# Taking the products that nobody reads out of TensorE's program, in the setup and at the change of layer

## The reference

```
x_n = x_flat / max(norm(x_flat over pixels), 1e-12)
cos = einsum('bcn,bdn->cd', x_n, x_n) / 32
idx = top_k(-abs(cos).T, 2)               # each channel's partner
gs, gsq = sums and square sums of a channel and its partner
x = gamma * (x - mean) * rsqrt(var + eps) + beta
```

```
off1 = make_offset(conv3x3(x, tm1_w, tm1_b), conv3x3(x, tr1_w, tr1_b))
out = relu(batchnorm(deform_conv(x, off1, dcn1_w), bn1_g, bn1_b))
off2 = make_offset(conv3x3(out, tm2_w, tm2_b), conv3x3(out, tr2_w, tr2_b))
out = batchnorm(deform_conv(out, off2, dcn2_w), bn2_g, bn2_b)
return relu(out + x)
```

## Time and profile before

| | before |
|---|---|
| median of 3 runs | 448.58 us (447.6 to 449.65) |
| profiled execution | 447.31 us, of which the span is 445.4 us |
| TensorE busy | 415.5 us, 93% of the span, 7435 records |
| ScalarE, VectorE busy | 318.5 us (72%), 313.4 us (70%) |
| GpSimd busy | 110.6 us (25%) |
| mean granted TensorE clock | 0.990 |

### The profile page before, as it was taken

How to read it: one execution, slowest core, us unless ns; L and a number is a source line. 1 busy time by engine, 2 the same in 40 slices (tenths; PEclk the granted TensorE clock), 3 DMA queues, 4 the chain that set the end, 5 groups by cost and what they waited for, 6 DMA issues and landing times.

```text
span 445.4 us, 18471 instructions
## 1 busy us (share of the span) xinstructions
PE 415.5 (93%) x7435; PEld 308.0 (69%) x7435; DVE 313.4 (70%) x865; ACT 318.5 (72%) x385; POOL 110.6 (25%) x241
## 2 busy tenths in 40 slices
PE   5978999999999999999988999999999999999970
PEld 4755677777777777777865677777777777777860
DVE  4657977777787777776429877877777777777435
ACT  2536787777887777777726788777877778777735
POOL 6203422222222222208002322222222212210000
PEclk9999999999999999999999999999999999999996
DMA  7202332222211122212000242212222222221005
GB/s 224 69 2 45 55 47 44 48 45 45 45 35 30 35 45 45 46 37 39 3 1 6 54 82 37 36 34 44 45 45 45 44 42 41 43 48 37 3 3 189
DMA packets 59385, 20.72 MB, mean 47 GB/s; under 512 B 51680, under 2 KB 59184, under 8 KB 59344
## 3 DMA queue, kind: packets, MB, share of 16 engines
q1 hardware_dynamic: 54464, 17.75, 19.4%
q0 software_dynamic: 4880, 2.37, 2.2%
HBM read 3.24 MB, written 2.10 MB: 12 GB/s over the span
## 4 chain that ended last, share of the span: by engine, by line
PE 88%; ACT 4%; DVE 4%; DMA 1%; issue 1%; SPq 0%; DVEq 0%; ACTq 0%
PE acc_ps L672 57%; PE z_ps L649 13%; PE build_ps L633 10%; PE side_ps L585 3%; PE side_ps L595 2%; ACT S L454 1%; DMA xs<-in_x 1%; PE side_ps L575 1%; ACT raw L507 1%; DVE bstats L764 1%; PE side_ps L615 1%; PE acc_ps L542 1%; PE build_ps L532 1%; ACT conv_sb L431 0%; ACT Z L447 0%
## 5 line engine op out<-in xcount | busy, mean ns | idle before, releaser
L672 PE MATMUL acc_ps<-S,Z 64*64 64x256 f32 x4608 | 286.7, 376 | 1.1 <-ACT S L454 1.0
L454 ACT ACTIVATE S<-build_ps,minus 128x1024 f32<-128x1024 f32 x192 | 203.7, 1111 | 51.6 <-PE build_ps L633 50.7
L672 PEld LDWEIGHTS acc_ps<-S,Z 64*64 64x64 f32 x4608 | 193.7, 132 | 56.4 <-issue 3.8
L649 PE MATMUL z_ps<-wz,xflat 64*64 64x192 f32 x1536 | 109.6, 331 | 0.1
L895 DVE TENSOR_SCALAR S<-build_ps 128x512 f32<-128x512 f32 x96 | 66.1, 689 | 35.2 <-PE build_ps L633 35.1
L447 ACT ACTIVATE Z<-z_ps 128x768 f32<-128x768 f32 x96 | 77.9, 812 | 5.4 <-PE z_ps L649 5.4
L649 PEld LDWEIGHTS z_ps<-wz,xflat 64*64 64x64 f32 x1536 | 71.3, 132 | 12.5 <-issue 0.5
L265 POOL DMA_DIRECT2D moved<-conv_sb x140 | 70.8, 513 | 20.0 <-POOL conv_sb L354 15.8
L633 PE MATMUL build_ps<-feat_rows,cst 64*64 64x512 f16 x576 | 72.1, 381 | 2.9 <-ACT S L454 1.5
L897 DVE TENSOR_SCALAR S<-build_ps 128x512 f32<-128x512 f32 x96 | 65.3, 680 | 0.0
L902 DVE COPY raw<-acc_ps 128x256 f32 (+1 forms) x32 | 13.6, 424 | 67.2 <-PE acc_ps L672 67.2
(11 more groups left out here) (103 smaller groups left out, 260.7 us busy)
## 6 DMA issues: line engine op xcount, KB each, us to landing
xs<-in_x SPq DMA_DIRECT2D x4, 512.0 KB, 6.4
out<-raw SPq DMA_DIRECT2D x7, 256.0 KB, 2.5
moved<-conv_sb POOLq DMA_DIRECT2D x56, 11.2 KB, 1.7
moved<-conv_sb SPq DMA_DIRECT2D x56, 11.2 KB
moved<-conv_sb POOLq DMA_DIRECT2D x56, 11.3 KB, 1.7
wz<-in_dcn_w POOLq DMA_DIRECT2D x2, 288.0 KB, 4.7
feat_rows<-feats SPq DMA_TRANSPOSE x30, 3.7
moved<-conv_sb SPq DMA_DIRECT2D x28, 12.0 KB
```

The lines of the kernel that those rows point to most:

```text
L454: act.activation(S[:, (parity + b) % 2, half, 0:ACT_TAPS, :], build_ps[:, 0:ACT_TAPS, :], ACT.Relu, bias=minus2[:, :], scale=1.0 if half = ...
L649: mm = pe.matmul(z_ps[halves[c], i, h * BLOCK_COLS:(h + 1) * BLOCK_COLS], xflat[parity][halves[i], pixels], wz[halves[i], layer, h, b * BL ...
L672: mm = pe.matmul(acc_ps[halves[i], g, 0:HW], Z[halves[g], slot, i, half, j * C:(j + 1) * C], S[halves[g], slot, half, j, i * HW:(i + 1) * ...
```

## The change

All five calls of `keep_busy` and its definition are taken out. Nothing else is touched; ScalarE's, VectorE's, GpSimd's and SyncE's programs stay as they were.

```diff
@@ -512,12 +512,6 @@
             pe.wait_ge(ident_in, 16)
 
-            def keep_busy(count):
-
-                for n in range(count):
-                    pe.matmul(build_ps[:, BLOCK_TAPS - 1, 0:P], ident, ident, start=True, stop=True, skip_group_check=True)
-
-            keep_busy(10)
 
             def turn(j):
@@ -551,14 +545,12 @@
             pe.matmul(side_ps[:, 0, 0:C], fold, gram_sb[:, :], start=True, stop=True).then_inc(gram_step, 1)
-            keep_busy(6)
             pe.wait_ge(setup_dve, 8)
             pe.transpose(side_ps[:, 1, 0:P], pick[:, :], ident).then_inc(gram_step, 1)
             pe.wait_ge(setup_dve, 9)
             pe.wait_ge(sums_ready, X_CHUNKS)
             pe.matmul(side_ps[:, 0, 0:2 * PAIRS], pick_t[:, :], sums[:, :, :].rearrange("p a t -> p (a t)"),
                       start=True, stop=True).then_inc(gram_step, 1)
-            keep_busy(9)
             pe.wait_ge(weights_in, 16 * 9)
@@ -728,12 +720,8 @@
                 for_pairs(pe, first, body)
-                if layer == 0:
-                    keep_busy(4)
                 pe.wait_ge(bn_dve, BN_OPS * layer + 1)
                 pe.matmul(side_ps[:, 1, 0:2], fold, bmv[:, :], start=True, stop=True).then_inc(bn_folded, 1)
-                if layer == 0:
-                    keep_busy(8)
```

## The result

| | before | after |
|---|---|---|
| median of 4 runs each | 448.28 us (447.6 to 449.65) | 455.78 us (454.24 to 459.58) |
| ratio | | 1.0176, 95% interval 1.0107 to 1.0245 |
| profiled execution | 447.31 us, span 445.4 | 454.24 us, span 452.4 |
| mean granted TensorE clock | 0.990 | 0.965 |

What follows compares the result with a forecast made beforehand. TensorE, busy 415.5 of 445.4 us (93%), was taken to bound the kernel. Terms 0 + 1.7 + 0 + 2.0 + 2.0 = 5.7 us took the profiled 447.31 to 453.0, with 1.27 for the median 454.3; range 450.8 to 461.5.

Steps and rivals of the forecast that it cites:

- step 1: Setup's transposes and Gram products: they start at the low clock, so the last Gram product is 1.7 us late.
- Step 2: Chain from last Gram product to first convolution: clock falls in 6.66 us with three small products, at no cost.
- Step 3: Start of layer 0: cold from the first convolution, costing 2.0 us (bounds 0 and 4.5), nothing later giving it back.
- Step 4: Change of layer: 4.6 us with one tiny product drops the clock, at slightly better than even odds, costing 2.0 us.
- Direct gain: All five blocks: none delays a product that is read, so removing them gains zero directly (bounds 0 and 0.9 us).
- Rival (e): Layer starts: recovery is slow as waits break the work, 4.5 us in place of 2.0, twice: 459 us; chance 0.06.
- Rival (a): Change of layer: only the long setup stretch drops the clock, these 4.6 us do not: 3.7 us, 452.3; chance 0.18.
- Rival (b): Setup: transposes do not raise the clock, TensorE stays cold to its end: 10.0 or 12.0 us, 458.6 to 460.6; chance 0.31.
- (c): Both gaps: clock rises once with the first real work, then small products hold it: 1.7 us, 450.3; chance 0.08.
- (d): Setup and gaps: clock rises by itself at about 10 us and holds: 447.7 to 448.6 us; chance 0.05.

Runs made afterwards that it cites:

- e1: Kernel before with only the first block of ten unread products taken out: 449.28 us against 448.63, ratio 1.0008.
- e2: Kernel before without the second and third blocks, between the last Gram product and the first convolution: 452.5 us, ratio 1.0078.
- e3: Kernel before without the fourth and fifth blocks, at the change of layer: 453.2 us, ratio 1.0083.
- e5: Kernel before with only the second block (6 products behind the fold of the Gram matrix) taken out: 449.48 us against 447.9, ratio 1.0045.
- e8: Kernel before with only the fourth block (4 products ahead of the tiny fold at the change of layer) taken out: 449.69 us against 448.6, ratio 1.0017.
- e12: Kernel after, plus one unread product behind each of the first two convolutions of a layer: 455.69 us against 448.6 for the kernel before, ratio 1.0163.
- e7: Kernel before with only the fifth block (8 products behind the tiny fold at the change of layer) taken out: 452.35 us against 448.6, ratio 1.0105.
- e6: Kernel before with only the third block (9 products just ahead of the first convolution) taken out: 452.1 us against 447.9, ratio 1.0109.
- e4: Kernel before with all unread products replaced by twice as many unread transposes: 447.39 us against 448.63, ratio 0.9964.
- e11: Repeat run of the kernel before with all unread products replaced by twice as many unread transposes: 448.59 us against 448.6, ratio 1.0005.
- e9: Kernel before with unread products doubled in count and cut to two moving columns in place of 128: 468.39 us against 447.9, ratio 1.0449.
- e10: Kernel before with the first block moved ahead of all transfers, as 22 unread products of a zeroed tile: 447.54 us against 447.9, ratio 1.0005.

## Why the prediction was right

The direction, the mechanism and the three places were right, and 455.78 is 1.5 us above the forecast of 454.3. The sum was 5.7 us and the spans show 6.9. That it comes so near is in part luck: step 1 was too large by 0.6 us, steps 2 to 4 were too small by 1.9 in all, and the working of steps 3 and 4 does not hold, as told below.

*Direct gain, zero.* Right. From the last Gram product to the first convolution the kernel after takes 6.90 us, the one before 6.66, so nothing in front of the convolution came sooner, and no ratio of e1, e2, e3 and e5 to e8 is below 1.

*Step 1, 1.7 us.* Right in kind, too large: 1.08. The third turn is late by 0.30 (12.66 against 12.36) and not by 0.7, and the rest is 0.78 and not 1.0. The cold spans were a little shorter than the ratio of 1.83 gave (eight transposes 1.94, not 2.07; from 12.66 to 14.76 a pair takes 2.10 in place of 1.20, a ratio of 1.75), the first transpose came 0.1 earlier, and the rise was at about 14.7, 5.0 us after it, not 5.4.

*Step 2, a fall at no cost.* The fall came, at 25.0. The product with the sums was cold (0.64 for 0.41), so the first convolution is late by 0.24 more than the Gram products.

*Step 3, 2.0 us.* The lag grows by 2.75 us up to the first sample, and 0.32 of it is regained by the end of layer 0, so 2.43 stay. My sentence that nothing later gives any of it back was wrong by that much. Two things in the working were wrong. First, I let 5.4 us of the low level reach to the end of the second convolution. The cold work ahead of that convolution takes 5.3 us by itself (28.50 to 33.78), so my own figure would have kept only 0.87 + 0.47 + 0.63 - 0.2 = 1.8 us of TensorE's delay. The clock stayed low for longer, 6.7 us after the first convolution, and the second one was cold for most of its length: that made it 2.79 (second weighing 36.85 against 32.74, less 1.32). Second, I took TensorE's 0.38 us of slack ahead of the turn of the features off the delay. The chain does not run through that slack. ScalarE copies the second weighing's result (L447) and then, in its own order, the turned features (L475), for which the building waits. In the timelines of all engines of the kernel before and of the kernel after:

```profile
34.43 0.60 ACT L475 ACTIVATE feat_rows<-acc_ps 128x512 f16<-128x512 f32 x1
```

```profile
37.79 0.81 ACT L447 ACTIVATE Z<-z_ps 128x768 f32<-128x768 f32 x1 [1.10 <-PE z_ps L641]
...
38.50 0.59 ACT L475 ACTIVATE feat_rows<-acc_ps 128x512 f16<-128x512 f32 x1
```

The features' copy has no idle time ahead of it in either: it follows the copy of the weighing, which was released by TensorE. It is late by 4.07 us, as the first sample is, while the turn itself (37.66 against 34.00) is late by only 3.66.

*Step 4, 2.0 us.* A fall was given slightly better than even odds; it came in the profiles of the kernel after, of e3 and of e12, and after much shorter gaps in e7 and e8. The cost was 3.2 us (6.93 - 3.75), of which 0.1 is the cold fold. This is the most mis-sized term. It assumed the clock back 5.4 us after a layer's first convolution, a time read off the first block of plain products. The profile shows 6.7 us in layer 0 and 7.8 in layer 1, where the second convolution is cold to its end too, so that the delay up to the second weighing is 3.05 us; and again nothing is to be taken off for the slack. In e2 and e6 the clock took 12.7 and 11.6 us to come back. Rival (e), slow recovery, had 0.06 and was in part true: its 4.5 us for a layer's start is near the 4.8 and 4.2 that the stretch up to the first sample lost in e2 and e6.

*Rival (a)*, no fall at the change of layer: refuted by the profile and by e3. Its argument, that 4.6 us are less than the one stretch seen to suffice, was a weak one: 5.4 us was an instance and not a least value. In the kernel after the clock fell 2.2 us after the last sample (230.96 to 233.2).

*Rival (b)*, transposes do not raise the clock, 0.31: refuted twice. In the kernel after the clock rose amid the mix of transposes and Gram products, with 7 us of it still to do; in e4 and e11 it rose with nothing but transposes run. I gave it too much.

*Rivals (c) and (d)*: refuted by the two dips, and (d) also by the first transposes, which stayed cold until 14.7 us.

## What to carry to other kernels

Work that nobody reads can pay for itself through TensorE's clock: 74 records that cost nothing where they stood were worth 7 us. Look for it where TensorE stands idle ahead of a chain that waits on it; here the gaps were 6.7 us in the setup and 4.6 at the change of layer. Fill the whole gap, and first of all the part right ahead of the work: the third block saved more than the second, and the second and the fourth saved nothing that could be measured where their partners were missing. Let the filler end before the real work is due (e9). Read the clock from the durations of one form of product, not from the busy share: with two-column products TensorE was busy for 2.00 of 2.00 us at 0.50. And when a delay is followed through a chain, follow it on every engine: a slack ahead of one instruction is worth nothing if another engine's program order passes it by.

## What the runs showed of the hardware

- TensorE busy 2.00 of 2.00 us at a granted clock of 0.50 (e9): a stream of products with weight loads of 128 columns and two moving ones did not raise the clock in 8.7 us, and the clock fell at 28.2 us, 2.5 us into such a stream. Float32 transposes raised it and were followed by no fall (e4, e11), and products of zeros raised it (e10).
- The spacing of unread float32 products did not depend on the moving columns: 0.214 us a record at the low level with 2 columns, and 0.214 with 128.
- The clock fell 2.2 us after the last dense product in the kernel after (233.2 against 230.96), and 5.4 us after it at the end of the kernel before. After a gap of 2.3 us with one tiny product in it, it still fell 1.1 us into the next block (e8). The low level then lasted 3.4 us in e5 and e8, where a block of 128-column products was running, and 17 us in e2, where none was.
- After the same first block of plain products the clock rose at 7.7 us (e3), 8.0 (e5), 8.2 (e6), 9.9 (e7 and e8), 10.2 (before) and 13.9 (e2), where the first real transpose started between 9.5 and 10.9.
